# A recurrent gated model on one core: a second mixing product on GpSimd, history products in pieces, and a new order of work on all engines

## The reference

```python
encoded = tanh(xt @ We + st @ Ue + be)                       # 24 values
new_state = tanh(xt x Wx + st x Ws + bk)                     # 8 candidates of 32
mem = concatenate([[encoded, err]], mem[:-1])                # 20 entries of 25
a = relu(mem.reshape(b, -1) @ enc_w1 + enc_b1)
agent_in = relu(a @ enc_w2 + enc_b2)
h1, c1 = lstm_cell(agent_in, h1, c1, ...)
h2, c2 = lstm_cell(h1, h2, c2, ...)
gate = softmax(h2 @ gate_w + gate_b)
theta = clamp01(mean(abs(mem[:, :10, -1])) * 2.5)
gate = gate * theta + gs * (1 - theta)                       # gs: the gate as given
st = sum over c of gate[c] * new_state[c]
pred = clamp01(st[:, -1]);  err = pred - yt
```

## Time and profile before

| | |
|---|---|
| median of three runs | 5656.6 us (5656.21 to 5656.87) |
| profiled execution, first to last instruction | 5654.1 us |
| TensorE matmuls busy | 5444.6 us, 96% of the span |
| TensorE weight loads busy | 3397.7 us, 60% |
| VectorE busy | 4678.1 us, 83% |
| ScalarE busy | 3830.9 us, 68% |
| GpSimd busy | 1646.7 us, 29% |
| granted TensorE clock | 0.998 |
| state transposes (two an item) | 1024 |

### The profile page before, as it was taken

How to read it: one execution, slowest core, us unless ns; L and a number is a source line. 1 busy time by engine, 2 the same in 40 slices (tenths; PEclk the granted TensorE clock), 3 DMA queues, 4 the chain that set the end, 5 groups by cost and what they waited for, 6 DMA issues and landing times.

```text
span 5654.1 us, 184300 instructions
## 1 busy us (share of the span) xinstructions
PE 5444.6 (96%) x67584; PEld 3397.7 (60%) x67584; DVE 4678.1 (83%) x12841; ACT 3830.9 (68%) x9217; POOL 1646.7 (29%) x3589
## 2 busy tenths in 40 slices
PE   7999999999999999999999999999999999999998
PEld 4666666666666666666666666666666666666665
DVE  7888888888888888888888888888888888888887
ACT  5666666666666666666666666666666666666665
POOL 2222222222222222222222222222222222222222
PEclk9999999999999999999999999999999999999999
DMA  2111111111111111111111111111111111111111
GB/s 66 28 29 30 28 31 28 31 28 31 28 31 28 31 28 28 31 28 31 28 31 28 31 28 31 28 29 30 28 31 28 31 28 31 28 31 28 31 28 39
DMA packets 299286, 172.38 MB, mean 30 GB/s; under 512 B 156734, under 2 KB 263882, under 8 KB 298714
## 3 DMA queue, kind: packets, MB, share of 16 engines
q1 hardware_dynamic: 293568, 159.42, 10.8%
q10 hardware_dynamic: 5146, 3.66, 0.2%
HBM read 74.65 MB, written 2.10 MB: 14 GB/s over the span
## 4 chain that ended last, share of the span: by engine, by line
PE 69%; ACT 15%; DVE 12%; issue 4%; DMA 0%; POOL 0%; ACTq 0%; POOLq 0%; DVEq 0%
PE chain L412 17%; PE a_ps L374 10%; PE cand_ps L343 8%; PE cand_ps L334 8%; ACT a_sb L523 6%; PE chain L399 6%; PE a_ps L363 6%; ACT gates L548 5%; DVE cell_in L708 5%; DVE added L694 4%; PE chain L308 4%; PE a_ps L385 4%; PE chain L429 4%; PE cand_ps L329 3%; ACT tanh_c L554 3%
## 5 line engine op out<-in xcount | busy, mean ns | idle before, releaser
L363 PE MATMUL a_ps<-hist,w_hist 125*64 125x512 f16 x12288 | 1700.2, 381 | 24.9 <-DMA w_hist<-enc_table 24.9
L785 DVE TENSOR_REDUCE state<-mixed 128x64 f32<-128x512 f32 x2048 | 1352.6, 681 | 34.1 <-POOL mixed L873 0.7
L541 ACT ACTIVATE cand<-cand_ps 128x512 f32<-128x512 f32 x2048 | 1154.6, 590 | 184.8 <-PE cand_ps L343 184.8
L412 PE MATMUL chain<-cell_in,cell_w 128*64 128x128 f32 x16384 | 1092.8, 276 | 0.7 <-ACT cell_in L531 0.5
L412 PEld LDWEIGHTS chain<-cell_in,cell_w 128*64 128x64 f32 x16384 | 888.3, 136 | 288.2 <-ACT cell_in L531 181.5
L900 POOL TENSOR_TENSOR err_ring<-pred_now,ys 128x8 f32 x512 | 128.6, 251 | 3106.0 <-DVE pred_now L792 3106.0
L548 ACT ACTIVATE gates<-chain 128x512 f32<-128x512 f32 x1024 | 611.4, 597 | 619.8 <-PE chain L412 619.8
L363 PEld LDWEIGHTS a_ps<-hist,w_hist 125*64 125x64 f16 x12288 | 658.6, 110 | 447.2 <-issue 26.0
L554 ACT ACTIVATE tanh_c<-gates 128x128 f32<-128x128 f32 x1024 | 316.7, 309 | 690.0 <-DVE gates L700 690.0
L694 DVE SCALAR_TENSOR_TENSOR added<-gates 128x256 f32<-128x256 f32 x1024 | 435.5, 425 | 419.4 <-ACT gates L548 419.4
L708 DVE SCALAR_TENSOR_TENSOR cell_in<-gates,tanh_c 64x128 f32<-64x128 f32 x2048 | 588.0, 287 | 159.4 <-ACT tanh_c L554 145.6
(11 more groups left out here) (74 smaller groups left out, 6660.7 us busy)
## 6 DMA issues: line engine op xcount, KB each, us to landing
x_sb<-in_x_l SPq DMA_DIRECT2D x260, 256.0 KB, 2.8
hist<-entry_parts SPq DMA_DIRECT2D x2048, 25.0 KB
w_hist<-enc_table SPq DMA_DIRECT2D x258, 128.0 KB, 2.4
y_rows<-in_y_l SPq DMA_DIRECT2D x260, 8.0 KB
ys<-in_y ACTq DMA_DIRECT2D x1, 2048.0 KB, 16.3
preds_out<-preds SPq DMA_DIRECT2D x1, 2048.0 KB, 8.1
cand<-in_encoder ACTq DMA_DIRECT2D x1, 640.0 KB, 3.8
cell_w<-in_cell ACTq DMA_DIRECT2D x2, 256.0 KB, 4.8
```

Of the source, the lines that this page charges most:

```text
L363: nc.tensor.matmul(a_ps[g][ENC * half:ENC * half + ENC, :], w_hist[0:HROWS, w_slot(u), kk, wp, :], hist[0:HROWS, xp, k, at:at + 512], star ...
L412: last = nc.tensor.matmul(chain[g][rows, P * r:P * r + P], cell_w[c][:, hf, r, :], cell_in[c][:, g, hf, :], start=False, stop=True, skip_g ...
L541: ins = nc.scalar.activation(cand[:, g, q // 2, :, q % 2, :, :].rearrange("p h s c -> p h (s c)"), cand_ps[q][:, :].rearrange("p (h k) -> ...
L785: V.tensor_reduce(state[:, g, hf, 2 * pair:2 * pair + 2, :], mixed[:, pair, hf, :, :, :], AX, ALU.add)\
```

## The change

- GpSimd forms the product of quarter 0 too: `mix_quarter(item, q)` is called for quarters 1 and 0, with `kept_gate` of the next item between them, and `gate_in_sbuf` and `kept_share` ahead. `mix(., 0)` is no longer called on VectorE. The semaphore `q_mulpool` becomes two, one a quarter.
- A semaphore for each of the four sums (`q_sum[hf][pair]`), so that GpSimd's products wait for the sums of pair 0 alone.
- History blocks can be issued in pieces of one product (two matmuls): `history(item, kk, first, end)`.
- `candidates_bias` is split from `candidates_x`; `agent_input`, `next_hidden` and `new_hidden` take one half a call.
- A new order in `phase` on TensorE, ScalarE, VectorE and GpSimd. On TensorE the cut between phases moves too: the candidates' s products and the second cell of `old` stand at the head of a phase, and the transposes, encoder and first cell of `cur` follow.

The core of the diff:

```diff
 (TensorE)
-            def candidates_x(item, before, extra):
+            def candidates_bias(item):
+                for q in CAND_ORDER:
+                    pe.wait_ge(q_cand[q], n)
...
+            def history(item, kk, first=0, end=len(PIECES)):
...
             def phase(items, extra):
                 new, cur, old = items
                 if cur:
+                    history(cur, 1, 1, 3)
+                if old:
+                    candidates_s(old)
+                if cur:
+                    history(cur, 2, 0, 1)
+                if old:
+                    bias_of_cell(old, 1)
+                if cur:
+                    encoded_x(cur, extra)
+                if old:
+                    cell_gates(old, 1)
+                if cur:
+                    history(cur, 2, 1, 2)
+                    state_transpose(cur, 0)
+                    state_transpose(cur, 1)
+                    history(cur, 2, 2, 3)
+                    history(cur, 3, 0, 1)
+                if new:
+                    history_waits(new, extra)
+                    history(new, 0, 0, 1)
+                if cur:
                     encoded_s(cur)
+                    history(cur, 3, 1, 3)
                 if old:
                     logit_bias(old)
-                if cur:
-                    history(cur, 3)
+                if new:
+                    history(new, 0, 1, 2)
                 if old:
                     gate_logits(old)
                 if cur:
                     encoder1_now(cur)
+                    bias_of_cell(cur, 0)
+                    candidates_bias(cur)
+                if new:
+                    history(new, 0, 2, 3)
                 if cur:
                     encoder2(cur)
+                    candidates_x(cur)
                     cell_gates(cur, 0)
+                if new:
+                    history(new, 1, 0, 1)
...
 (ScalarE)
                 if cur:
-                    agent_input(cur)
+                    agent_input(cur, 1)
+                    cell_tanhs(cur, 0)
                 if old:
-                    next_hidden(old)
-                if cur:
-                    cell_tanhs(cur, 0)
+                    next_hidden(old, 1)
+                if cur:
                     value_tanh(cur, 0)
+                    candidates(cur, 0)
+                    candidates(cur, 3)
                     candidates(cur, 2)
-                    candidates(cur, 1)
                     cell_tanhs(cur, 1)
                 if new:
                     state_take(new)
                 if cur:
+                    next_hidden(cur, 0)
                     value_tanh(cur, 1)
                 if new:
                     at_least_zero(new)
                     encoded(new)
                 if cur:
-                    candidates(cur, 3)
+                    candidates(cur, 1)
                 if new:
                     entry_high(new)
                 if cur:
                     exponentials(cur)
                 if new:
                     encoder1(new)
-                if cur:
-                    candidates(cur, 0)
+                    agent_input(new, 0)
...
 (VectorE)
             def phase(items, extra):
                 new, cur, old = items
                 if cur:
-                    new_hidden(cur, 0)
-                if old:
-                    mix_sum(old, 0, 1)
-                    mix_sum(old, 1, 1)
-                if cur:
-                    error_sum(cur)
                     cell_terms(cur, 1)
                     cell_value(cur, 1)
                 if old:
                     prediction(old)
                 if cur:
-                    new_hidden(cur, 1)
+                    new_hidden(cur, 1, 0)
+                    new_hidden(cur, 1, 1)
                 if new:
                     errors(new, extra)
-                if cur:
-                    thetas(cur)
+                    error_sum(new)
+                if cur:
                     peaks(cur)
                     below_peak(cur)
+                if new:
+                    thetas(new)
+                if cur:
                     totals(cur)
                     reciprocals(cur)
                     shares(cur)
                     fresh_gate(cur)
                     new_gate(cur)
                     mix(cur, 1)
-                    mix(cur, 0)
-                    mix_sum(cur, 1, 0)
+                    mix_sum(cur, 1, 1)
+                    mix_sum(cur, 0, 1)
                 if new:
                     cell_terms(new, 0)
                     cell_value(new, 0)
+                    new_hidden(new, 0, 0)
+                    new_hidden(new, 0, 1)
                 if cur:
                     mix_sum(cur, 0, 0)
+                    mix_sum(cur, 1, 0)
...
 (GpSimd)
             def mix_quarter(item, q):
                 g, n, u = item
                 pool.wait_ge(q_keptfrom, n + GROUPS)
-                pool.wait_ge(q_cand[1], n)
+                pool.wait_ge(q_cand[q], n + 1)
 
                 for hf in range(HF):
-                    pool.wait_ge(q_sum[hf], SUMS * n + SUMS * (GROUPS - 1))
-                over_s = gate[:, g, 1:Q:2, :].rearrange("p h (o c) -> p h o c", o=1)\
+                    pool.wait_ge(q_sum[hf][0], n + (GROUPS - 1))
+                over_s = gate[:, g, q:Q:2, :].rearrange("p h (o c) -> p h o c", o=1)\
                     .to_broadcast([P, HF, S, C])
-                G.tensor_tensor(mixed[:, 0, :, 1, :, :], cand[:, g, 0, :, 1, :, :], over_s, ALU.mult)\
-                    .then_inc(q_mulpool, 1)
+                G.tensor_tensor(mixed[:, 0, :, q, :, :], cand[:, g, 0, :, q, :, :], over_s, ALU.mult)\
+                    .then_inc(q_mulpool[q], 1)
...
             def phase(items, extra):
                 new, cur, old = items
                 if old:
-                    mix_quarter(old)
+                    gate_in_sbuf(old)
+                if cur:
+                    kept_share(cur)
+                if old:
+                    mix_quarter(old, 1)
+                if cur:
+                    kept_gate(cur)
+                if old:
+                    mix_quarter(old, 0)
+                    keep_prediction(old, extra)
                     new_error(old, extra)
-                    keep_prediction(old, extra)
-                if cur:
-                    kept_share(cur)
-                    kept_gate(cur)
                 if new:
                     entry_low(new)
-                if cur:
-                    gate_in_sbuf(cur)
```

More of the change, by code:

```diff
@@ L147, in recurrent_kernel @@
                                     "ring", "predout"))
-        q_sum = [sem(f"q_sum{hf}") for hf in range(HF)]
+        q_sum = [[sem(f"q_sum{hf}_{pair}") for pair in range(2)] for hf in range(HF)]
         block = ctx.enter_context(nc.Block())
@@ L286, in state_transpose @@
                 g, n, u = item
-                pe.wait_ge(q_sum[hf], SUMS * n)
+                for pair in range(2):
+                    pe.wait_ge(q_sum[hf][pair], n)
                 last = nc.tensor.matmul(chain[g][:, P * hf:P * hf + P],
@@ L298, in x_wait, with encoded_x @@
                     pe.wait_ge(s_x[x_slot(u)], extra[0][u] if extra else 16)
-            def encoded_x(item, before, extra):
+            def encoded_x(item, extra):
                 g, n, u = item
                 x_wait(item, extra)
-                if before:
-                    for pair in MIX_ORDER:
-                        pe.wait_ge(q_mul[pair], before[1] + GROUPS if pair == MIX_ORDER[1] else before[1])
+                pe.wait_ge(q_mul[1], n)
                 for rows in ENTRY_ROWS:
@@ L346, in candidates_s, with history_waits @@
                 last.then_inc(q_candps, 1)
-            def history_waits(item, before, extra):
+            def history_waits(item, extra):
                 g, n, u = item
@@ L353, in history_waits @@
                     pe.wait_ge(s_hist[g], extra[2][u])
-                if before:
-                    pe.wait_ge(q_in, before[1])
-            def history(item, kk):
+            def history(item, kk, first=0, end=len(PIECES)):
                 g, n, u = item
                 k = HT - 1 - kk
-                for t, (wp, xp) in enumerate(((0, 0), (1, 0), (0, 1))):
+                for t in range(first, end):
+                    wp, xp = PIECES[t]
                     for half in range(2):
@@ L524, in encoder1, with agent_input @@
                     .then_inc(q_a, 1)
-            def agent_input(item):
+            def agent_input(item, hf):
                 g, n, u = item
-                act.wait_ge(q_inps, n)
-                for hf in range(HF):
-                    rows = AGENT_ROWS[hf]
-                    last = nc.scalar.activation(cell_in[0][rows, g, hf, :], a_ps[g][rows, 0:P], ACT.Relu,
-                                                bias=enc2_bias[rows, 0:1])
-                last.then_inc(q_in, 1)
+                rows = AGENT_ROWS[hf]
+                if hf == 0:
+                    act.wait_ge(q_inps, n)
```

(23 more changed lines are left out.)

78 lines of the change are left out of this document (35 added, 43 removed).

## The result

| | before | after |
|---|---|---|
| median of the runs | 5656.5 us | 5691.0 us |
| profiled execution | 5654.1 us | 5689.8 us |
| VectorE busy | 4678.1 us | 4418.9 us |
| GpSimd busy | 1646.7 us | 2232.2 us |
| ScalarE busy | 3830.9 us | 3865.3 us |

The kernel after takes 1.0059 times as long, 95% interval 1.0045 to 1.0074: it is slower by 34 us, and the interval leaves out 1. The forecast was slower by 69 us (5726 us). So the direction was forecast and the size is half of it, but the loss did not come about as forecast.

What follows compares the result with a forecast made beforehand. The prediction took a ring of five links, one packed by TensorE and four set by latency, as the bound. Links of 10.83 us plus 0.25 for blocking made 11.08 a phase against 10.946: 5726 us, range 5590 to 5800.

Steps and rivals of the forecast that it cites:

- The ring of five links: One phase as a closed chain, one stretch packed by TensorE and four set by latency; 10.946 us, 511 times.
- first to second gates: TensorE from first cell's gates to second's: candidate bias and x products leave, 3.54 us from 3.75, gain 0.21.
- Head and tail: Some 28 us before and 32 us behind the phases, counted as unchanged to within 2 us.
- the block: VectorE's `added` of the first cell waits for GpSimd's second product reading SBUF: 0.25 us late a phase.
- The first link: Second gates through logits to encoder 1 on TensorE: 4.10 us against 4.05 before, set by the state path.
- step 1: TensorE's prices for candidates x and s products: 0.86 and 0.96 us, with 0.10 for a change of tile.
- encoder 2 to first gates: TensorE link into which the candidates' x products move: 1.32 us against a latency of 1.28.
- Encoder 1 to encoder 2: TensorE link where the latency of 1.86 us holds, with about 1.85 of work to fit: 1.87.
- step 2: GpSimd's second product was to end 9.44 us behind the second gates, bounds 9.20 and 9.80.
- seams: Joints between blocks of TensorE work, estimated at 0.02 us each, upper bound 0.10.
- TensorE becomes the bound: Rival: six extra seams at 0.10 us each make TensorE's phase 11.2 us, 5786 us; chance 0.10.
- No blocking: Rival: GpSimd's second product does not delay `added`, or ends first; phase 10.83 us, 5597 us; chance 0.30.

Runs made afterwards that it cites:

- the idle addition: The kernel after with one unused GpSimd addition of 256 elements, two inputs in SBUF, behind its second product: 5867.9 us.
- first experiment: The kernel after with the candidates' x products moved directly in front of their s products, three history pieces in their old place: 5611.2 us, 0.9919 of before.

## Why the prediction was wrong

**Right.** The ring of five links is what sets the time, 511 times the phase. The gain was expected in first to second gates, and that is where most of it is. Head and tail were right. Pieces of one shape that follow each other still cost 0.22 each (three in 0.67).

**Luck.** That the sign came out right is luck. The forecast had a gain of 0.12 us a phase on TensorE and a loss of 0.25 by the block. The runs show a loss of 0.07 on TensorE and no block.

The first link came near too (4.03 for 4.10), by another path than the forecast had. The prediction let the tanh of `entry` and 0.12 of waiting set it. But `encoded_s` came 0.20 earlier than forecast, and encoder 1 only 0.07. In both kernels encoder 1 starts 0.15 behind the end of `errors`, which VectorE begins 0.03 behind the second cell's hidden values (before, then after):

```profile
2811.36 0.42 DVE L687 SCALAR_TENSOR_TENSOR entry<-clamped,y_rows 4x256 f32<-4x256 f32 x1
```

```profile
2810.91 0.42 DVE L704 SCALAR_TENSOR_TENSOR entry<-clamped,y_rows 4x256 f32<-4x256 f32 x1
```

So the second cell's latency sets this link, 3.43 to 3.44 us to the end of its hidden values, and not the path through the transposes.

**Wrong, step 1: the price of a block of 32-row tiles.** The prediction knew of changes of tile and gave 0.10 to each, from the 0.96 of the s products over 0.86 of the x products. But that row shows only what a block pays when another shape follows. What it pays when another shape stands ahead was hidden in the kernel before: the x products' weights were loaded while the bias matmuls of the same tile shape ran. In the kernel after the x products have no such neighbour, and the loads start with the matmuls (weight loads of the x products; before, whose matmuls start at 2805.40, and after, whose matmuls start at 2813.73, one phase behind those shown):

```profile
2805.18 0.85 PEld L334 LDWEIGHTS cand_ps<-w_x,x_sb 32*128 32x128 f32 x16
```

```profile
2813.73 0.74 PEld L334 LDWEIGHTS cand_ps<-w_x,x_sb 32*128 32x128 f32 x16 [0.20 <-issue]
```

The first four of the sixteen matmuls are longer, as the line of the x products shows (ns min/median/max; before and then after, 2800 to 2900 us):

```profile
L334 PE MATMUL cand_ps<-w_x,x_sb x144: 374/374/375, 2805.4 to 2893.6; 32*128 32x256 f32 x144
```

```profile
L334 PE MATMUL cand_ps<-w_x,x_sb x144: 374/374/478, 2802.7 to 2891.5; 32*128 32x256 f32 x144
```

So a block that stands alone takes 1.08: 0.10 of it for its long first matmuls and 0.11 for the change behind it. The prediction counted the second and not the first, 0.96 for each of the two blocks. (The 0.10 that it gave to the change ahead of the s products lies in the history block there, which takes 0.75 for three pieces and not 0.67.) The Trainium skill, "TensorEngine Tiling (Array Packing)", section "Key Properties", says that a change of tiling mode drains TensorE. The traces agree as far as they show it: the block behind a change starts 0.09 to 0.12 us late.

The terms: encoder 2 to first gates 1.43 for 1.32, by the x products. First to second gates 3.64 for 3.54, which was the latency; by the prediction's own list of TensorE's work it was 3.47, and the runs have 0.12 more in the s products and 0.06 more in the first gates (0.92 for 0.86, though the earlier trace rows has 1.03 with a change behind them). Encoder 1 to encoder 2 1.90 for 1.87, where the candidate bias makes a third group between tiles of other shapes. Less the 0.07 of the first link, the phase is 11.00, where the forecast without its block was 10.83: the change costs 0.07 us a phase where 0.12 was expected as its gain ahead of the block. That this grouping is the cause is shown by taking one group away (80 us less), by cutting it again (168 us more, without the piece itself) and by moving the bias (17 us less).

**Wrong, step 2: where GpSimd's second product ends.** Forecast 9.44 behind the second gates, measured 9.09 (2805.54 less 2796.45, the second gates one phase of 11.00 before 2807.45). Three terms were too large: encoded_s starts at 2.22 and not 2.42, because the two transposes took 0.37 and not 0.52 and the 0.05 for seams was not there; `gate` to first product 0.47 and not 0.58, for a reason that the runs don't show; `kept_gate` 0.22 and not 0.24. `added`, forecast ready at 9.04, was ready at 9.13, for the most part since step 1 made its gates late (7.36 for 7.29). The forecast overlap of 0.40 us became a miss of 0.04. Some 0.15 of the 0.52 for the transposes was no work of TensorE: in the kernel before the second one starts 0.05 behind the end of the last sum, which it waits for.

```profile
2807.79 1.28 DVE L785 TENSOR_REDUCE state<-mixed 128x64 f32<-128x512 f32 x2
...
2809.12 0.33 PE L288 MATMUL chain<-ident,state 128*128 128x128 f32 x1
```

In the kernel after a history piece stands ahead of the transposes and fills that wait.

**The mechanism of step 2** was right though idle: when the product or the idle addition is there, `added` ends 0.28 or 0.29 behind it. It had a second side that I did not see. Whether the two instructions meet depends on how fast TensorE gets to the first gates, so that each loss makes the other smaller: a slow TensorE hides the block. The prediction added the block to a ring that it had counted too fast.

**Of the rivals,** "TensorE becomes the bound" was the one that came true, with the 0.10 chance; its reason (seams) was the wrong one, and its time, 5786 us, was far too high. "No blocking" was true in its condition, not in its time of 5597 us. The best kernel here reaches that time, 5594 us, but only because x and s products stand together in it and one more change of tile is gone.

**Open.** That the transposes take 0.37 for 0.52 was not tried by itself; it is read from the timelines alone. The new orders on ScalarE and VectorE were not undone one by one.

## What to carry over

Count on TensorE by groups of equal tile shape, not by matmuls: in this kernel a block of sixteen matmuls in 32-row tiles that stands alone costs 0.22 us more than one between its like, which is a quarter of its work. Ahead of a forecast, ask of each block whether the row it is priced from had a neighbour of its own shape on either side. And check for each pair of VectorE and GpSimd instructions that read SBUF whether a faster neighbour would bring them together: the margin here was 0.04 us, and in the run that made the product 0.6 us later it cost 174 us in all.

## What the runs showed of the hardware

- A GpSimd product or addition that reads SBUF holds up a VectorE scalar_tensor_tensor with two SBUF inputs that comes later, until the GpSimd instruction ends; the held one is recorded with its wait inside its duration (0.81 and 0.83 us for 0.43) and ends 0.28 or 0.29 us behind the release. A GpSimd fill of 0.53 us did not hold it (0.43).
- Behind a block of another tile shape, the first four of the sixteen fp32 matmuls in 32*128 tiles are recorded with 478 ns in place of 374 (kernel after); the whole block of sixteen takes 1.08 us alone (kernel after), 0.96 or 0.97 with a like neighbour on one side (kernel before, first experiment), 0.86 in the middle (kernel before).
- Two sums (tensor_reduce) of VectorE beside GpSimd's product took 1.28 us together in the kernel after, what two take there without it.
